# Rounds of a graph layer with one scan per group in feature-major form

## The reference

```python
counts = segment_sum(ones, seg_ids, N_SUP)          # seg_ids is all zeros here
h = pooled / maximum(counts, 1.0)[:, None]          # row 0: the mean over all nodes, other rows zero
def prop(z):
    return segment_sum(edge_weight[:, None] * z[src], dst, num_segments=N_SUP)
for i in range(5):
    x_start = prop(h @ W[i] + b[i])
    xi = h
    for _ in range(5):
        xi = (prop(xi) + x_start) / (2.0 + 0.9)
    mean, var = jnp.mean(xi, axis=0), jnp.var(xi, axis=0)
    out = gamma[i] * (xi - mean) / sqrt(var + 1e-5) + beta[i]
    h = where(out > 0, out, 0.01 * out)
return h[seg_ids]                                   # row 0 for every node
x = _layernorm(x + ...)                             # after each of the four blocks
```

## Time and profile before

| what | us |
|---|---|
| median of 3 runs | 9781.79 |
| lowest and highest of the 3 | 9777.96, 9782.67 |
| span of the profiled execution | 11994.1 |

### The profile page before, as it was taken

How to read it: one execution, slowest core, us unless ns; L and a number is a source line. 1 busy time by engine, 2 the same in 40 slices (tenths; PEclk the granted TensorE clock), 3 DMA queues, 4 the chain that set the end, 5 groups by cost and what they waited for, 6 DMA issues and landing times. The chain is left out here.

```text
span 11994.1 us, 149789 instructions
## 1 busy us (share of the span) xinstructions
PE 6782.4 (57%) x33931; PEld 5074.2 (42%) x33931; DVE 6277.9 (52%) x20811; ACT 1432.6 (12%) x3027; POOL 6513.3 (54%) x6508
## 2 busy tenths in 40 slices
PE   3544547665567656567656667655567266570072
PEld 2333214443356444356443446544346144560051
DVE  5576545555545555545555554555554755550067
ACT  0022003000002000001100000200000500351005
POOL 4667351555643556553455654356554555676646
PEclk8755767766677766667776667776667577785555
DMA  3143001344422344421334431334431511692106
GB/s 121 38 159 122 2 2 54 70 82 83 84 47 65 69 79 84 82 56 40 87 76 83 84 63 30 92 73 84 83 72 31 181 48 52 146 200 37 24 20 267
DMA packets 526027, 950.80 MB, mean 79 GB/s; under 512 B 187011, under 2 KB 269788, under 8 KB 525604
## 3 DMA queue, kind: packets, MB, share of 16 engines
q0 software_dynamic: 192000, 330.22, 18.4%
q1 hardware_dynamic: 316196, 516.19, 13.8%
q10 hardware_dynamic: 17664, 102.61, 2.1%
HBM read 502.28 MB, written 458.64 MB: 80 GB/s over the span
## 5 line engine op out<-in xcount | busy, mean ns | idle before, releaser
L965 POOL DMA_INDIRECT G<-tab,gidx x4000 | 3805.8, 951 | 3554.8 <-issue 1897.5
L1401 PE MATMUL PS<-G,M 128*128 128x128 f32 x8000 | 2131.7, 408 | 1945.6 <-DVE G L396 1626.8
L1401 PEld LDWEIGHTS PS<-G,M 128*128 128x128 f32 x8000 | 1722.9, 276 | 2402.2 <-DVE G L396 1827.1
L1386 PE MATMUL PS<-G,lring 128*1 128x128 f32 x8000 | 1498.3, 348 | 224.9 <-DMA G<-tab,gidx 184.4
L398 DVE SCALAR_TENSOR_TENSOR G<-G,whole,PS 1x128 f32<-1x128 f32 (+1 forms) x3300 | 1103.5, 334 | 823.7 <-issue 128.2
L1346 DVE TENSOR_TENSOR Y<-PS,big 128x512 f32<-128x512 f32 x800 | 553.4, 692 | 1334.0 <-remote 1079.2
L419 DVE TENSOR_SCALAR M<-keyrow,keycol,wccol 128x128 f32 (+1 forms) x4004 | 1135.3, 364 | 29.3 <-issue 8.2
L1386 PEld LDWEIGHTS PS<-G,lring 128*1 128x1 f32 x8000 | 719.6, 100 | 779.7 <-DMA G<-tab,gidx 226.7
L1355 ACT COPY big<-PS 128x512 f32 x200 | 117.0, 585 | 5453.5 <-remote 3647.8
L1397 PE MATMUL PS<-M,G 128*128 128x128 f32 x1600 | 486.3, 401 | 437.9 <-DVE G L396 431.6
L1066 POOL DMA_INDIRECT Y<-pair_d,G x400 | 402.3, 1006 | 359.7 <-DMA pair_d<-UT 207.4
(11 more groups left out here) (498 smaller groups left out, 11639.0 us busy)
## 6 DMA issues: line engine op xcount, KB each, us to landing
tab<-Y SPq DMA_DIRECT2D x1000, 256.0 KB
big<-agg SPq DMA_DIRECT2D x90, 832.0 KB, 12.7
G<-tab,gidx POOLq DMA_INDIRECT x4000
big<-x SPq DMA_DIRECT2D x60, 832.0 KB, 8.8
xt_d<-big SPq DMA_DIRECT2D x30, 858.0 KB, 13.6
x2n<-big ACTq DMA_DIRECT2D x30, 838.5 KB
big<-x2n SPq DMA_DIRECT2D x30, 838.5 KB
agg<-big ACTq DMA_DIRECT2D x30, 832.0 KB
```

The costliest lines, as they stand in the source:

```text
L965: pool.indirect_dma_start(G[:, t % RG, 0:D], None, tab_in(k), bass.IndirectOffsetOnAxis(ap=gidx[:, t:t + 1], axis=0)).then_inc(l_got[t % R ...
L1386: nc.tensor.matmul(PS[0:1, CAR, j, :], lring[:, GR * h + j:GR * h + j + 1], G[:, s, 0:D], start=True, stop=True).then_inc(l_row, 1)
L1401: ins = nc.tensor.matmul(PS[:, SUM + h, j, :], M[:, GR * h + j, :], G[:, s, 0:D], start=True, stop=True)
```

## The change

Layers 1 to 4 are made anew. The gathered rows are turned to feature-major form, and the running sums go by one `tensor_tensor_scan` of 512 columns per group: state = keep flag x state + row, feature by feature, the keep flag (one byte in `keyrow`) being zero where a new node's run starts. Weights are multiplied in beforehand. The ring has five groups (RG = 20).

- The turn is gone. Round k = 4 stores its rows as they are to tabs[2], and round k = 0 gathers them from there. In it PE turns each gathered tile, ACT normalises while it copies the result out of PSUM (`turned_act`), DVE makes the leaky step, multiplies by the weights (`WR`, a row of 512 weights on all partitions, 256 KB loaded by SP for each group, and `QR`) and scans; PE turns back with `wplus` as the matrix and adds the bias by a matmul of `QR` and `BD` (512 columns). x_start's matmuls with W stay, with the nodes' leaky step on DVE added (`leaky_nodes`). The power is queued on POOL behind the first four gathers.
- Rounds k = 1 to 3: ACT multiplies each gathered tile by its column of weights (`weighted_rows`), PE transposes four tiles, DVE scans out of PSUM, PE transposes four tiles back with the plain identity, DVE adds `zt`.
- Round k = 4: the same up to the scan; ACT copies the sums to `zt` and the rows to `Y` (`kept_act`), SP stores them, DVE multiplies by (keep flag of the next position - 1) and takes `bn_stats`, which `totals` puts together for mean and variance. `node_sums` goes.
- The masks, the row matmuls, the one-row operations and the aggregation go.
- The expansion of layer 0 makes, beside the matmul of 512 columns, four of 128 columns per group, which DVE copies to `Y` and SP stores to tabs[2].
- `keyrow` gets the keep flags at the block's start (3.2 MB) and the destinations again in the second norm pass after the layers. The last row is gathered. Some buffers are laid over others.

```diff
-RG = 16
-NG = RG // GR
+NG = 5
+RG = NG * GR
@@ expansion, on PE, DVE
-                nc.tensor.matmul(bank(q), rows4[0:3, 0:D], Y[0:3, GR * q:GR * q + GR, :].rearrange("p s f -> p (s f)"),
-                                 start=True, stop=True).then_inc(o_ex, 1)
+                nc.tensor.matmul(bank(g % 2), rows4[0:3, 0:D], c, start=True, stop=True)
+                for j in range(GR):
+                    ins = nc.tensor.matmul(PS[:, 2 + g % 2, j, :], c[:, P * j:P * j + P], rows4[0:3, 0:D],
+                                           start=True, stop=True)
+                ins.then_inc(o_ex, 1)
...
+                nc.vector.tensor_copy(group_of(Y, g % NG), PS[:, 2 + g % 2, :, :]).then_inc(o_en, 1)
@@ l1_gather, on POOL
-                if t >= RG and t % U == 0:
-                    free = g0 + (t - RG) // GR + 2
-                    steady(pool, free, OPS * free + 1)
-                    pool.wait_ge(l_sum, free)
-                    pool.wait_ge(l_ch, OPS * free + 1)
+                n = t // GR
+                if t % U == 0 and n >= NG - 1:
+                    free = round_of(l, k) * GPR + n - NG + 4
+                    steady(pool, free)
+                    pool.wait_ge(l_ft, free)
+                if k == 0 and t == GR:
+                    inverse_deviation(pool, l)
@@ ACT, rounds 1 to 4 and round 0
+                ins = nc.scalar.activation(G[:, s, 0:D], G[:, s, 0:D], ACT.Copy,
+                                           scale=wz[:, bass.ds((NB * i + q) * GR + j, 1)])
...
+                nc.scalar.activation(M[:, GR * h:GR * h + GR, :], PS[:, FT_[h], :, :], ACT.Identity,
+                                     bias=tcol[:, 0:1], scale=scol[:, 0:1]).then_inc(l_he, 1)
@@ PE, forward and backward
+                    ins = nc.tensor.transpose(PS[:, FT_[h], j, :], G[:, s, 0:D], ident[:])
+                ins.then_inc(l_ft, 1)
...
+                if k == 0:
+                    pe.wait_ge(l_wc[q % NG], 32 * (NB // NG * NI * (l - 1) + NB // NG * i + q // NG + 1))
+                    nc.tensor.matmul(bank(BK_[h]), QR[:, q % NG, :], BD, start=True, stop=False)
+                    for j in range(GR):
+                        ins = nc.tensor.matmul(PS[:, BK_[h], j, :], UR[h][:, j, :], wplus[:], start=False,
+                                               stop=j == GR - 1)
+                else:
+                    for j in range(GR):
+                        ins = nc.tensor.transpose(PS[:, BK_[h], j, :], UR[h][:, j, :], ident[:])
@@ DVE
+                if k == 0:
+                    dve.wait_ge(l_he, n + 1)
+                    nc.vector.scalar_tensor_tensor(half, half, 0.01, half, ALU.mult, ALU.max).then_inc(l_lr, 1)
+                    if not is_last(i, q):
+                        leaky_nodes(i + (q + 1) // NB, (q + 1) % NB)
+                    dve.wait_ge(l_lr, n + 1)
+                    dve.wait_ge(l_wc[q % NG], 32 * (NB // NG * NI * (l - 1) + NB // NG * i + q // NG + 1))
+                    nc.vector.tensor_tensor(half, half, WR[:, q % NG, :], ALU.mult).then_inc(l_mu, 1)
+                    dve.wait_ge(l_mu, n + 1)
+                else:
+                    dve.wait_ge(l_ft, g + 3)
+                dve.wait_ge(l_bk, g + 1)
+                dve.wait_ge(l_sc, g + 2)
...
+                nc.vector.tensor_tensor_scan(S[h], keyrow[:, bass.ds(tile * P, GR * P)],
+                                             half if k == 0 else bank(FT_[h]), S[1 - h][:, GR * P - 1:GR * P],
+                                             ALU.mult, ALU.add).then_inc(l_sc, 1)
...
+                    nc.vector.scalar_tensor_tensor(mk, keyrow[:, bass.ds(tile * P + 1, GR * P)], 1.0, S[h],
+                                                   ALU.subtract, ALU.mult).then_inc(l_mk, 1)
+                    dve.wait_ge(l_mk, n + 1)
+                    nc.vector.bn_stats(stL[:, bass.ds(NB * i + q, 1), :].rearrange("p a b -> p (a b)"),
+                                       mk).then_inc(l_bn, 1)
@@ SP
+            sp.dma_start(WR[:, c, :], w_d[bass.ds(tile * P, GR * P)].partition_broadcast(P)).then_inc(l_wc[c], 16)
+            sp.dma_start(QR[0:GR, c, :], q_d.rearrange("(t f) -> t f", f=P)[bass.ds(tile, GR), :]).then_inc(l_wc[c], 16)
```

More of the change, by code:

```diff
@@ L901, in build @@
         zt = big[:, 0:T * D]
[L902 to L905, removed]
+        UR, HTR = (UO, UT), (OT, HT)
+        FT_, BK_, ZB_ = (0, 1), (2, 3), (4, 5)
+        GPR = T // GR
         l_got = pool_sems("l_got", RG)
-        l_u, l_h, l_hc, l_z, l_za, l_hz = (sems("l_" + n, 2) for n in "u h hc z za hz".split())
-        l_tab = sems("l_tab", NG)
+        l_g0 = pool_sems("l_g0", 1)[0]
+        l_w, l_wr, l_base, l_m, l_rows, l_keep, l_pad, l_first = (
+            sem("l_" + n) for n in "w wr base m rows keep pad first".split())
+        l_ft, l_sc, l_bk, l_ev, l_dg, l_he, l_mu, l_lr, l_hl, l_hc, l_z, l_za, l_zc, l_xc, l_mk, l_bn, l_bn2, l_st, l_col, l_pw = (
+            sem("l_" + n) for n in "ft sc bk ev dg he mu lr hl hc z za zc xc mk bn bn2 st col pw".split())
+        l_tab, l_wc = sems("l_tab", NG), sems("l_wc", NG)
+        S = [u[:].rearrange("p s f -> p (s f)") for u in UR]
+        QR = cf[:, 0:NG * P].rearrange("p (r f) -> p r f", r=NG)
+        BD = cf[:, NG * P:NG * P + GR * P]
         def tab_in(k):
@@ L913, in tab_out, with round_of @@
         def tab_out(k):
-            return tabs[2] if k < 0 else tabs[k % 2]
-        def round_no(l, k):
+            return tabs[2] if k == NL - 1 else tabs[k % 2]
+        def round_of(l, k):
             return (l - 1) * NL + k
[L921 to L941, removed]
+        def group_of(ring, q):
+            return ring[:, GR * q:GR * q + GR, :]
+        def zt_at(tile):
+            return zt[:, bass.ds(tile * D, GR * D)]
         def rows_of(tab, tile):
             return tab.rearrange("(p t) f -> p t f", t=T)[:, bass.ds(tile, GR), :]
[L947 to L951, removed]
+        def every_group(eng):
+            with eng.Fori(0, NI) as i:
+                for q in range(NB):
+                    yield i, q
@@ new lines, in lagged, with group_no, stores_before @@
+        def lagged(eng, one, two):
+            one(0, 0)
+            with eng.Fori(0, NI - 1) as i:
+                for q in range(NB):
+                    one(i + (q + 1) // NB, (q + 1) % NB)
+                    two(i, q)
+            for q in range(NB):
+                if q < NB - 1:
+                    one(NI - 1, q + 1)
+                two(NI - 1, q)
+        def group_no(l, k, i, q):
+            return round_of(l, k) * GPR + NB * i + q
+        def stores_before(l, k, i, q):
+            return 2 * NI * (round_of(l, k) + 1) + NB // NG * i + q // NG
@@ L965, in l1_gather @@
                 pool.indirect_dma_start(G[:, t % RG, 0:D], None, tab_in(k), bass.IndirectOffsetOnAxis(
                     ap=gidx[:, t:t + 1], axis=0)).then_inc(l_got[t % RG], 16)
[L969 to L975, removed]
-            return zt[:, bass.ds((RG * i + GR * q) * D, GR * D)].rearrange("p (s f) -> p s f", f=D)
-        def two_ahead(eng, one, two):
-            for q in range(2):
-                one(0, q)
-            for i, q in group_loop(eng):
-                if not (isinstance(i, int) and i == LI):
-                    one(i + (q + 2) // NG, (q + 2) % NG)
-                two(i, q)
```

495 lines of the change are left out of this document (253 added, 242 removed).

## The result

| kernel | median us | runs | ratio to before |
|---|---|---|---|
| before | 9779.88 | 4 (9771.07 to 9782.67) | |
| changed | 9706.78 | 4 (9698.51 to 9717.15) | 0.9923, 95% interval 0.9909 to 0.9938 |

The change gains 73 us where 300 were forecast. The direction and the range (9200 to 9720) held; the size is wrong by a factor of four. On a second chip the changed kernel had 0.991 of before (0.9893 to 0.9926), so the size is no accident of one chip. The time of before itself differed between sets of runs, from 9780 to 9612 us, and on one chip from 9644 to 9612.

A forecast was written before the change was run, and what follows sets the result against it. Ordinary rounds were taken as bound by POOL's gathers, 200 x 1.25 = 250 us. Turn -337, last round -72, expansion +85, keys and ends +24 gave -300: 9782 - 300 = 9482, rounded to 9480 us; range 9200 to 9720.

The forecast's parts named there:

- late signals: Waits on "remote" signals beside gathers in the profile, 1079.2 us on sums of k = 0 to 3; mostly absent from ordinary runs.
- The turn: Between layers, merged into k = 0: -264 us for layers 2 to 4, -73 in layer 1, together -337.
- the expansion: Layer 0, four more matmuls of 128 columns a group on PE: +85 us, between +43 and +104.
- The middle rounds: k = 1 to 3: all new work lies beside the gathers, the round stays at 250 us: 0.
- The keys: Keep flags loaded at the start, 15 us (0 to 28); keys reloaded in the second norm pass, 5 us (0 to 15).
- DVE is just under the pace, so 255 us for before and after: 0: Round k = 0: DVE needs 4.8 us a group, gathers 5.0; change 0, between -15 and +60 us a round.
- rival 2: DVE operations with two SBUF inputs lock POOL out: k = 0 +620 us, last round +120, 10220 us; chance 0.08.
- I take 268: Last round, k = 4: 268 us before, 250 after, -18 x 4 = -72 us, between 0 and -200.
- The check: Sum of what ordinary runs lack against the profiled span: 2192 of 2212 us, with last round at 268, 300 us guessed.
- rival 3: PE stays cold in k = 0: 6.2 us a group, +240 us, 9720 us; chance 0.12.
- the ring of five groups hides: In k = 0, 256 KB of weights a group share the store's queue; stores wait perhaps 1 us, hidden by the ring.
- Rival 1: Gathers cheaper in ordinary runs, say 1.15 us; change gains in every round, 240 us more, 9240 us; chance 0.18.

The follow-up runs named there:

- before_beside: The kernel before, unchanged, profiled again on the same chip as the changed kernel: 9613.49 us, profiled span 9611.7 us.
- after_beside: The changed kernel, unchanged, profiled on the same chip as the kernel before: 9535.31 us, profiled span 9533.5 us.
- neither edit: Changed kernel with k = 0's scan reading PSUM: 0.988 of before; or with k = 0's weights loaded for each layer's first five groups only: 0.991.

## Why the prediction was wrong

**What held.** The reading of the profile: late signals that ordinary runs don't have, and a kernel that is bound by 200 gathers of 1.25 us in every round. The turn (-325 measured, -337 forecast) and the expansion (+85.5, +85) are right to a few per cent. The middle rounds did not move; their gaps are longer by 1.3 us each; ACT's step is new in that chain, which may be why. The keys cost 4 us at the start and nothing that shows behind the last gather, where 20 were allowed.

**The step that failed first: "DVE is just under the pace, so 255 us for before and after: 0".** k = 0 costs 155 us. Of these 139.4 us lie in the rounds and 15.4 in longer gaps behind them, which no run takes apart. The mechanism in the rounds was rival 2, and it was put at 0.08 for two reasons. Its evidence against was POOL's equal busy time in k = 3 and k = 4 of the profile before (190.72, 190.64). That is a sum over 200 gathers, in an execution where hardly any square could hold one: of the 73 gathers that began during a square in its four last rounds, 68 did so in the first 0.05 us, where none is held (0.946 us on average), and only 5 later, at 1.18 to 1.27 us. The undisturbed profile of before (before_beside) has 190.97 us in k = 3 and 194.35 in the stretch of k = 4, less 0.56 for the power 193.8; two of its rows show why:

```profile
2811.96 0.69 DVE L1341 TENSOR_TENSOR OT<-Y 128x512 f32<-128x512 f32 x1
2812.10 1.39 POOL L965 DMA_INDIRECT G<-tab,gidx  x1 [0.30 <-issue]
```

A gather that began 0.14 us into the square ends 0.84 us after it. Even the first profile held this: the longest gather of k = 4 there is 1267 ns beside a median of 952, as its line's durations show:

```profile
L965 POOL DMA_INDIRECT G<-tab,gidx x200: 946/952/1267, 3383.9 to 3796.4; - x100
```

The prediction read the sum where the longest was wanted. And the rival's price was wrong too: it held POOL for the whole length of each operation, 155 us a round. The measured price follows from the rule of the rows: a gather pays only if it begins inside, and then what is left less 0.19 us (less 0.13 in the shorter operations, 0.95 less 0.82, whose first 0.05 us cost nothing). With a start every 1.25 us a scan costs (1.28 - 0.19)^2 / 2 / 1.25 = 0.48 us a group and each operation of 0.69 us costs 0.10 by either figure; with three of these that is 0.78 x 50 = 39 us, near the 34.9 us by which a round grew (139.4 / 4). Gather by gather, what is over 0.948 us in the four rounds of after_beside adds up to 103 us in scans, 33 in leaky steps and 4 in products. Priced so, rival 2 would have given 4 x 39 = +156 us in k = 0, on top of the forecast about 9640 us.

**The second: the last round, "I take 268".** Before, it is 252.5 to 257.1 us: PE's 301.40 busy us at a clock of 0.74 are 246.47 at 0.92, under the pace, as this line of before_beside shows (k = 4 alone):

```profile
2786.50:3043.60 257.10, 246.47 (x1917) 221.02 (x1917) 194.85 (x572) 28.13 (x48) 193.76 (x200) 0.92 0.31 51
```

The gain there is 6 us, not 72. The check that seemed to support 268 held a guess of 300 us for three other stages, and so could not tell 268 from 254: "It is no proof of the pace", it said. Nothing in it spoke against the lower end, 0.

These two terms are 155 + 66 = 221 of the 222 us between forecast and measured sum. The smaller misses cancel: turns +12, middle rounds +8, keys and ends -19.

**Where the range held by luck.** 9706.78 lies 13 us under its upper end, 9720. That end was drawn for rival 3, a cold PE, which did not come; what came was rival 2, which the range was meant to leave out, at a quarter of the price that the prediction gave it.

**What else the experiments corrected.** That "the ring of five groups hides" the loads is true only while gathers are held; with the scan's hold gone the product waits up to 5.9 us for them. Rival 3 (PE cold in k = 0) did not come: the clock is 0.86 there. Rival 1's cheaper gathers did not come either: 0.95 us and 0.305 between two are as profiled.

## What to carry to other kernels

Contention is read from single instructions, not from a round's mean: look for the longest of the instruction in question and for what ran when it began. Before an operation is placed beside indirect gathers, count its operands in SBUF; if one of them can be left in PSUM, the gathers keep their pace. And where one bound is lifted, measure the next two together: here the lock hid late loads, neither edit brought more than 0.3% alone, and both gave 1.1%: 0.9797 of before with the weights spread by PE, and 0.9786 with the expansion's transposes.

## What the hardware showed that was not expected

A held gather ends a fixed time after the DVE operation that held it, 0.757 us after a scan and 0.82 us after other forms, to within 0.01 us. A gather that begins in the first 0.05 us of a leaky step or a product is not held. An operation that reads the same tile twice (the leaky step, M with M) holds it like two different tiles. The masks of the kernel before (L419) hold gathers too, though they read one tile and two columns of SBUF: in before_beside 131 gathers that began in one took over 0.99 us, 1.08 at most, and ended 0.82 us after it. So one tile in SBUF is no assurance for every form, and no run here parts the forms. DVE is never lengthened by it: 1.28 us with gathers held, 1.28 without. The same program took 9780, 9644, 9620 and 9612 us in four sets of runs.
